# The seam from the attention half to the MLP half of an adaLN, gated-scan and feed-forward kernel: where the MLP's preparation is placed, and the order of its first products

## What is computed

```python
y    = clip((x * styles) @ weight.T * dcoefs + bias)          # modulated projection
h    = rms_norm(y) * norm_w
gate = gelu(h @ fc_gate_w.T + b);  hs = h @ fc_w.T + b
r, i = sigmoid(h @ fc_r_w.T + b), sigmoid(h @ fc_i_w.T + b)
a    = exp(-8 * softplus(alpha) * r);  s = sqrt(1 - a * a) * hs * i
out  = scan(o = a_t * o + s_t)                                 # along the tokens
hs2  = out * gate + y
h2   = rms_norm(hs2) * norm2_w
x1   = x + (gelu(h2 @ mlp_gate_w.T + b) * (h2 @ mlp_fc_w.T + b)) @ out_w.T + out_b + hs2
return x1 + quantised_ffn(conditioned_mlp(x1, ...))            # third part, not touched
```

## Time and profile before

| | us |
|---|---|
| median of 3 runs | 1930.0 |
| the three runs | 1926.86, 1930.0, 1933.8 |
| the profiled execution, its own time | 1932.52 |
| its span, from the first to the last instruction | 1930.4 |
| mean granted TensorE clock | 0.983 of full |

### The profile page before, as it was taken

How to read it: one execution, slowest core, us unless ns; L and a number is a source line. 1 busy time by engine, 2 the same in 40 slices (tenths; PEclk the granted TensorE clock), 3 DMA queues, 4 the chain that set the end, 5 groups by cost and what they waited for, 6 DMA issues and landing times.

```text
span 1930.4 us, 23556 instructions
## 1 busy us (share of the span) xinstructions
PE 1850.1 (96%) x8374; PEld 1491.1 (77%) x8374; DVE 1010.2 (52%) x1650; ACT 763.6 (40%) x1154; POOL 383.1 (20%) x340
## 2 busy tenths in 40 slices
PE   7999999999899999999999999997899999999996
PEld 6788888888688888888888888766677777777774
DVE  6656665657543333233333333257675575675665
ACT  6555555546422222222212221234353453554543
POOL 0111111222000000000000000033264464464432
PEclk9999999999899999999999999998899999999997
DMA  5011111005301010101010101433022122122201
GB/s 188 1 44 44 43 43 44 23 1 196 109 1 66 1 66 0 67 0 66 1 67 1 66 1 66 147 135 128 21 78 89 55 78 88 54 78 88 65 13 42
DMA packets 55184, 114.05 MB, mean 59 GB/s; under 512 B 4226, under 2 KB 4482, under 8 KB 55092
## 3 DMA queue, kind: packets, MB, share of 16 engines
q1 hardware_dynamic: 49956, 95.00, 14.0%
q0 software_dynamic: 4608, 16.78, 2.8%
q10 hardware_dynamic: 528, 1.05, 0.2%
HBM read 87.65 MB, written 25.17 MB: 58 GB/s over the span
## 4 chain that ended last, share of the span: by engine, by line
PE 84%; DVE 6%; issue 3%; DMA 3%; ACT 1%; POOL 0%; DVEq 0%; ACTq 0%; SPq 0%; POOLq 0%
PE bank L802 27%; PE bank L281 17%; PE bank L817 14%; PE bank L1421 10%; PE bank L1456 4%; PE bank L1438 4%; PE bank L267 3%; DMA x_tiles<-x_d 2%; PE bank L1369 1%; PE bank L1378 1%; DVE operand_parts L1918 1%; DVE operand_full L1908 1%; PE bank L1385 1%; PE bank L831 1%; DVE stats L1878 1%
## 5 line engine op out<-in xcount | busy, mean ns | idle before, releaser
L281 PE MATMUL bank<-h_parts,gate_w 128*128 128x512 f32 x1536 | 356.0, 393 | 0.1
L281 PEld LDWEIGHTS bank<-h_parts,gate_w 128*128 128x128 f32 x1536 | 289.3, 188 | 64.5 <-issue 4.5
L1011 DVE SCALAR_TENSOR_TENSOR product_full<-bank,vec_sb,gelu 128x512 f32<-128x512 f32 x96 | 72.0, 750 | 435.4 <-PE bank L802 375.3
L817 PE MATMUL bank<-mlp_out_w,product_parts 128*128 128x512 f32 x1152 | 286.2, 398 | 10.0 <-DVE product_parts L1014 10.0
L1421 PE MATMUL bank<-operand_parts,int_w 128*128 128x512 f32 x1152 | 288.5, 396 | 6.9 <-DVE operand_parts L1918 6.5
L802 PE MATMUL bank<-h_parts,mlp_gate_w 128*128 128x512 f32 x1152 | 277.2, 389 | 1.2 <-DVE h_parts L996 1.2
L802 PE MATMUL bank<-h_parts,mlp_fc_w 128*128 128x512 f32 x1152 | 276.8, 389 | 0.0
L817 PEld LDWEIGHTS bank<-mlp_out_w,product_parts 128*128 128x128 f32 x1152 | 215.6, 189 | 62.7 <-issue 17.1
L1421 PEld LDWEIGHTS bank<-operand_parts,int_w 128*128 128x128 f32 x1152 | 216.9, 190 | 54.1 <-issue 5.1
L802 PEld LDWEIGHTS bank<-h_parts,mlp_gate_w 128*128 128x128 f32 x1152 | 216.4, 188 | 46.9 <-issue 2.0
L802 PEld LDWEIGHTS bank<-h_parts,mlp_fc_w 128*128 128x128 f32 x1152 | 216.2, 188 | 44.9
(11 more groups left out here) (255 smaller groups left out, 2280.6 us busy)
## 6 DMA issues: line engine op xcount, KB each, us to landing
xin<-xT SPq DMA_DIRECT2D x8, 1024.0 KB, 7.0
hs_d<-u SPq DMA_DIRECT2D x8, 1024.0 KB, 5.1
x_tiles<-x SPq DMA_DIRECT2D x8, 1024.0 KB, 5.5
x_d<-x_tiles SPq DMA_DIRECT2D x8, 1024.0 KB, 4.5
x_tiles<-x_d SPq DMA_DIRECT2D x8, 1024.0 KB
out<-u_tiles SPq DMA_DIRECT2D x32, 256.0 KB, 2.0
raw_w<-int_W SPq DMA_DIRECT2D x7, 1024.0 KB, 7.9
x_residual<-x_d SPq DMA_DIRECT2D x28, 256.0 KB, 3.6
```

The source lines that it names most:

```text
L281: i = pe.matmul(bank[:], gw[:, w, s, k, m * P:(m + 1) * P], hr[:, q, t, k, :], start=k == 0 and n == 0, stop=k == KT - 1 and n == 2)
L817: i = pe.matmul(A[t][:], pr[:, j % 2, s, t * P:(t + 1) * P], ow[j // KT][:, w, j % KT, :], start=j == 0 and n == 0, stop=j == FT - 1 and n ...
L1011: dve.scalar_tensor_tensor(out=pf[:], in0=FB[j % 2][:], scalar=v("mlp_fc_b", j), in1=gg[:], op0=ALU.add, op1=ALU.mult).then_inc(p_full, 1)
```

## The change

On SP, the load of hs2 block 0 is taken out of `early` into `early_block`, which is called one block earlier, in the body of block 6, ahead of the wait for and the store of that block. Its two waits (h_high, h_low of all blocks) go with it.

The preparation on ScalarE, VectorE and TensorE moves one gate tile ahead: ScalarE splits chunk 0 after gate tile 0, takes the root and splits chunk 1 after tile 1, and makes h's high parts after tile 2; VectorE adds the squares after tile 0, splits chunk 0 and normalises after tile 1, splits chunk 1 and makes h's low parts after tile 2; TensorE's mean square stands ahead of gate tile 2. ScalarE's split of chunk 2 moves from behind the attention's last add to ahead of the attention's four gelus (`early(4)`), VectorE's moves behind product tile 0 of the MLP.

The waits between the halves change: ScalarE's `first` waits for the attention's last product out * gate (`og_done`) alone, VectorE's waits for nothing. TensorE waits for the last two u tiles ahead of the first two fc products, which write their banks.

In block 0 alone, the list `BEHIND` says which output products follow product pair j: none behind pairs 0 and 1, number 0 behind pair 2, numbers 1 and 2 behind pair 3, and from pair 4 on number j - 1 as before.

```diff
--- before.py
+++ after.py
@@ -201,7 +201,8 @@
         MS0 = R[0]
         XP = [xr, hr[:, 1]]
         mlp = following(sems, {"projected": y_ps, "h_high": h_high, "h_low": h_low, "hs": hs_ps, "r": r_ps, "i": i_ps,
-                               "gates": g_ps, "added": hs2_done, "stored": hs2_stored, "gelu": g_evac})
+                               "gates": g_ps, "added": hs2_done, "stored": hs2_stored, "gelu": g_evac,
+                               "product": og_done, "u": u_done})
 
         @block.sync
         def _(sp):
@@ -210,11 +211,13 @@
                     sp.wait_ge(x_low, KT * b)
                 sp.dma_start(xin[:], xT[:, :, bass.ts(b, BT)]).then_inc(x_loaded, 16)
 
-            early, run = mlp["sync"](sp)
+            early_block, early, run = mlp["sync"](sp)
 
             def body(b, q, nxt, nxt2):
                 if nxt2:
                     load(b + 2)
+                elif nxt:
+                    early_block()
                 if not nxt:
                     early()
                 sp.wait_ge(hs2_done, KT * (b + 1))
@@ -314,7 +317,7 @@
                 if nxt:
                     mean_square(b + 1)
                 for m in range(1, KT):
-                    if not nxt and m == 3:
+                    if not nxt and m == 2:
                         early()
                     gates(b, q, m)
                 if isinstance(b, int) and b == 0:
@@ -435,6 +438,8 @@
                     act.wait_ge(a_sq, KT * b + m + 1)
                     act.activation(a2[:, m, :], a2[:, m, :], ACT.Sqrt, scale=-0.25,
                                    bias=quarter).then_inc(q_done, 1)
+                if not nxt:
+                    early(4)
                 for m in range(KT):
                     act.wait_ge(g_ps, KT * b + m + 1)
                     act.wait_ge(og_done, KT * b + max(m - 1, 0))
@@ -720,6 +725,7 @@
     SQ = 5
     MS = 8
     T_AT = {4: 0, 5: 1}
+    BEHIND = [(0, 0), (0, 0), (0, 1), (1, 3)] + [(j - 1, j) for j in range(4, FT)]
     T = [G[0], G[1], G[0], FB[0]]
     last_of = {"gate": g_ps, "fc": f_ps, "out": o_ps, "tokens": t_ps, "x1": r1, "hs2": r2, "stored": x_stored,
                "product": p_full, "gelu": g_evac, "h_full": h_full, "h_high": h_high, "h_low": h_low, "mean": ms_ps}
@@ -741,10 +747,12 @@
             src, raw = chunks[n][0:2]
             sp.dma_start(raw, src).then_inc(w_loaded[n], 16)
 
-        def early():
+        def early_block():
             sp.wait_ge(att["h_high"], KT * NB)
             sp.wait_ge(att["h_low"], KT * NB)
             load(0, 0)
+
+        def early():
             sp.wait_ge(att["projected"], KT * NB)
             load_weights(0)
             load_weights(1)
@@ -778,7 +786,7 @@
             blocks(sp, first, body)
             last_run()
 
-        return early, run
+        return early_block, early, run
 
     def tensor_program(pe):
         last_early, ready, tokens, last_run = ffn["tensor"](pe, last_of, FB)
@@ -846,6 +854,8 @@
                     pe.wait_ge(p_full, FT * b)
                 if nxt and j == MS:
                     pe.wait_ge(rms, b + 2)
+                if not prev and j < 2:
+                    pe.wait_ge(att["u"], KT * NB - 1 + j)
                 if not nxt:
                     ready(j)
                 product(b, FB[j % 2], 1, j, f_ps)
@@ -857,8 +867,8 @@
                 if not nxt:
                     pe.wait_ge(p_full, LAST + j)
                     last_early(j)
-                if j >= 1:
-                    project_out(b, prev, j - 1)
+                for n in [j - 1] if prev and j else range(*BEHIND[j]) if not prev else []:
+                    project_out(b, prev, n)
             for t in range(2, TT):
                 if not nxt:
                     ready(FT)
@@ -935,18 +945,17 @@
             if m == 0:
                 act.wait_ge(att["projected"], KT * NB)
                 squares(0, 0)
+                split_high(0)
             elif m == 1:
-                split_high(0)
-            elif m == 2:
                 root(0)
                 split_high(1)
-            elif m == 3:
+            elif m == 2:
                 h_parts(0)
+            elif m == 4:
+                split_high(2)
 
         def first():
-            act.wait_ge(att["added"], KT * NB)
-            split_high(2)
-            act.wait_ge(att["stored"], 16 * NB)
+            act.wait_ge(att["product"], KT * NB)
 
         def run():
             blocks(act, first, body)
@@ -1013,6 +1022,8 @@
                 dve.wait_ge(p_high, FT * b + j + 1)
                 dve.tensor_tensor(pr[:, j % 2, 1, :], pf[:], pr[:, j % 2, 0, :].bitcast(F32),
                                   ALU.subtract).then_inc(p_low, 1)
+                if not prev and j == 0:
+                    split_low(NEXT - 1)
                 if not prev and NEXT + j < len(chunks):
                     split_low(NEXT + j)
                 if nxt and j == SQ + 1:
@@ -1035,18 +1046,17 @@
                 dve.tensor_tensor(xt[:, t, :], A[t][:], xt[:, t, :], ALU.add).then_inc(r1, 1)
 
         def early(m):
-            if m == 1:
+            if m == 0:
                 add_squares(0)
+            elif m == 1:
                 split_low(0)
+                normalise(0, 0)
             elif m == 2:
-                normalise(0, 0)
                 split_low(1)
-            elif m == 3:
                 h_low_part(0)
 
         def first():
-            split_low(2)
-            dve.wait_ge(att["stored"], 16 * NB)
+            pass
 
         def run():
             blocks(dve, first, body)
```

## The result

| | before | changed |
|---|---|---|
| median, 5 runs each on one chip | 1930.0 us | 1915.7 us |
| lowest and highest | 1926.86, 1933.8 | 1913.56, 1920.41 |
| ratio, 95% interval | | 0.993 (0.9909 to 0.9952) |
| profiled execution, its own time | 1932.52 | 1914.22 |
| span | 1930.4 | 1912.3 |

The change is faster by 14.3 us in the medians; the interval allows 9 to 18 us. The last two rows split the difference of the profiled executions: 13.1 us lie at or ahead of gate product 4, where the change is, and 5.0 us behind it.

A forecast was written before the change was run, and what follows sets the result against it. TensorE was taken as the bound, busy 1850.1 of 1930.4 us. The seam's 12.96 us, less 0.2 for the mean square and 0 to 0.2 for gate 2, gave 12.7: 1930.0 to 1917.3 us, range 1912 to 1924.

The forecast's parts named there:

- The seam: From the MLP's first gate product to gate product 4: 42.88 us where 29.92 would do, a loss of 12.96 us.
- the low clock: Behind TensorE's idle stretch ahead of the first output product: half clock, costing 2.98 us.
- rival 3: Between the halves: gelu 0 or output 0 still depends on something late, like the store; gain only 2.3 us; chance 0.05.
- The tail of the attention: VectorE's work from 469.50 on comes 2 to 3 us earlier; last out * gate ends at 478.5 to 479.3.
- the spare ahead of gate product 2: MLP start: gelu 0 is ready 2.1 us before gate product 2 needs it, or 0.2 short in the bad bound.
- The mean square: Last attention block: TensorE, one gate tile earlier, waits 0 to 0.4 us for VectorE's adds; 0.2 taken.
- late bound: Gate weights for ScalarE's split of chunk 0: taken to land at 441.75, at the latest 445.69.
- the delay allowed for: ScalarE's split of chunk 2: weights landing up to 471.7 would delay the attention's first gelus by 3.0 us.
- rival 2: Last attention block: a late transfer or add holds TensorE at the mean square; gain 7.5, about 1922.5 us; chance 0.06.
- rival 4: Last attention block: block 6's store landing over 10 us later holds the mean square, making the whole slower; chance 0.03.
- Nothing behind gate 4 changes: Rest of the kernel after gate product 4: clock full, TensorE dense, everything merely follows 12.7 us earlier.

## Why the prediction was right

**The terms.** The seam was costed at 12.96 us, and 12.96 went. Its parts were cut slightly wrong: from start to start TensorE stood still for 491.95 - 479.09 - 2.72 = 10.14 us and not 9.98, and the low clock cost 2.8 and not 2.98 (the two products behind the idle time took 5.26 and 3.00 us). The sum is the same. The prediction had a price for the third pair without the waits (rival 3, a gain of 2.3); the run gave 2.74. It had none for the waits without the third pair. The runs take the change apart in steps:

| kernel | seam, us |
|---|---|
| before | 12.96 |
| the waits | 7.99 |
| the waits, chunk 2 at its new place | 6.45 |
| the same and the preparation ahead | 2.72 |
| the same and the third pair (the whole change) | 0 |
| the third pair alone | 10.22 |
| waits, chunk 2 and third pair, preparation at its old place | 0.37 |

So the place of chunk 2 is a third ingredient beside the waits and the pairs, worth 1.5 us in the row where it is seen alone. The prediction counted it in its chain (low parts of chunk 2 behind product 0) but gave it no term. Waits and third pair with chunk 2 at its old place were not run. In the kernel with the waits alone, gelu 0 ended at 484.47 and gate product 2 would have had its turn at 482.2, so about 2.3 us would have been left there, an estimate from these rows.

**The tail of the attention.** Predicted for the last out * gate was 478.5 to 479.3, measured 479.00; for gelu 0 479.7, measured 479.72; for the spare ahead of gate product 2 2.1 us, measured 1.96, and 0.2 short if the tail did not move, measured 0.4. The inputs of outputs 0, 1 and 2 came as counted: low parts of chunk 2 at 484.36 for 484.4, parts of product 1 at 489.06 for 489.3, of product 2 at 493.78 for 494.2.

**The mean square.** Predicted was a wait of 0 to 0.4 us, with 0.2 in the sum. The adds ended at 441.84 + 0.69 = 442.53, 2.77 us after VectorE's last step of tile 0 (439.34 + 0.42); the contended row of the kernel before gave 2.82. TensorE's matmul row has no idle time at all; its weight load shows 0.23 us. The term was up to 0.2 us too large.

By the Trainium skill, "SBUF — State Buffer", Who interferes with whom, the first add, the square and two adds stand end to end, which makes 3.1 us as an estimate. The trace agrees in kind and came out 0.3 us shorter.

**What landed when.** The gate weights were guessed to land at 441.75 with a late bound of 445.69; ScalarE's wait ended at 441.46. Chunk 2's weights were there at 468.60, when ScalarE was ready for them, so the delay allowed for was not needed.

**The size of the low clock.** This was mis-sized in the rivals, though not in the forecast. Rivals 2, 3 and 4 were charged 2.98 us each, and rival 2 as soon as TensorE had idled for 2.5 us. Measured, each in one execution but the 6.2, were 0.1 behind 2.42 us of idle, 1.6 behind 3.07, 1.6 behind 4.67, 2.8 behind 5.36, 1.65 and 1.7 behind 6.2, 2.5 behind 7.52 and 2.8 behind 9.98. Rival 2's total was not far off all the same (5.5 predicted for a delay of 2.5, 4.7 measured for 3.07 and its low clock), because the wait was longer and the low clock shorter.

**The number.** The forecast of 1917.3 us lies 1.6 above the median of the changed kernel and 0.1 above that of its second measurement, 1917.18. The gain is the fairer measure, since the kernel before stood at 1930.0 in the one group and 1927.91 in the other: 12.7 was predicted, 14.3 and 10.7 were measured. That the forecast lies so near the middle is in part luck; what is shown is that the seam gave 12.96. For the profiled execution 1919.8 was predicted and 1914.22 measured. Of the 18.1 us by which its span was shorter, 13.1 lie up to gate product 4, 0.6 in the MLP between that and its last block and 4.4 in the third part, where the kernels are the same. "Nothing behind gate 4 changes" held for the kernel, and a single execution still moved by 5 us there.

## What to carry to other kernels

At a seam between two parts, look for the one element-wise step that waits for a store which its data don't need, and narrow the wait to what its buffer really overlaps. That alone gave less than half here. Take what else stands on the chain off it (here the split of chunk 2, 1.5 us), and reorder the long work on the busiest engine so that it covers what is left. All of it together closed the gap; no part alone did. Steps that feed a matmul placed ahead in that engine's queue must be ready by then, so the load that starts them belongs to the same edit. And price an idle stretch of TensorE with the slow matmuls behind it, as a range and not as one number.

## What the runs showed of the hardware that was not expected

The low clock behind an idle TensorE isn't ordered by the length of the idle time in these profiles: 5.36 us of it cost 2.8 us, and 6.2 us cost 1.65 and 1.7 in two executions. In the third part of the kernel, waits of about 1 us are followed by slow matmuls in some executions (granted clock 0.72, 1.5 us more) and not in others (1.00), and the time behind the seam spreads over 5 us for kernels that are the same there.

VectorE's four scalar_tensor_tensor operations on two SBUF inputs took 3.51 us in the changed kernel (446.66) instead of 2.73 in the kernel before (449.36), where no GpSimd operation ran beside them. GpSimd's square beside them took 1.48 us, and 1.04 where it was alone. In the kernel with the waits alone the same meeting with GpSimd's adds cost 1.4 us on the critical chain.
